# The once-only part of a graph network kernel, cut into 86 pieces that run between the steps of the first graphs

## The reference

```python
# layer 0: pair scores over all nodes, normalised over the whole matrix, leaky relu, softmax over axis 1
e = (x @ a_i)[:, :, None] + (x @ a_j)[:, None, :]
e = leaky((e - mean) * rsqrt(var + eps) * adj + adj);  h = sigmoid(softmax(e, axis=1) @ x)
# layer 1: graph attention, then a GIN step
h = x @ Wp + bp;  s = leaky(h @ a_src [:, None] + h @ a_dst [None, :]);  s = where(adj <= 0, -max, s)
h_gat = relu(layernorm((softmax(s) * adj) @ h));  h_gin = (1 + eps) * h_gat + adj @ h_gat
z = relu(layernorm(h_gin @ W1 + b1));  out = relu(z @ W2 + b2 + h_gat)
# layer 2: weights of the edges from a table e[256], by each edge's number in adj
A = softmax(where(adj > 0, e[number of the edge], NEG), axis=1)
out = (A * eye) @ (x @ W[0]) + (A * (1 - eye)) @ (x @ W[1]) + bias
# layer 3: graph attention with self-loops added to adj
out = elu(softmax(where(adj + eye == 0, -1e9, leaky(e_src + e_dst))) @ (x @ W))
```

## Time and profile before

| | us |
|---|---|
| median of 3 runs | 1245.51 (1245.16 to 1245.55) |
| the profiled execution | 1249.84 |
| its span, first to last instruction | 1248.1 |
| PE busy | 1111.1 (89%) |
| DVE busy | 1096.2 (88%) |
| ACT busy | 1020.0 (82%) |
| POOL busy | 449.1 (36%) |

### The profile page before, as it was taken

One profiled execution on the slowest core, in us unless ns is written; L12 is line 12 of the kernel. 1 busy time (PEld: TensorE's weight loads), 2 busy tenths in 40 slices (PEclk: granted clock), 3 DMA queues, 4 the chain that ended last, 5 costly groups with the idle time before them and its releaser, 6 DMA issues.

```text
span 1248.1 us, 29006 instructions
## 1 busy us (share of the span) xinstructions
PE 1111.1 (89%) x7632; PEld 903.1 (72%) x7632; DVE 1096.2 (88%) x4212; ACT 1020.0 (82%) x2582; POOL 449.1 (36%) x832
## 2 busy tenths in 40 slices
PE   6447889999999999999999999999999999999863
PEld 3235677888777777778877777777888777778753
DVE  5656789999999999999999999999999999998743
ACT  2244679999999888998999988889999999889764
POOL 4002324343334343444333334434443334443320
PEclk9667999999999999999999999999999999999986
DMA  3000001101100111111011011111101100110000
GB/s 64 17 26 9 27 26 35 35 26 34 34 22 20 34 34 34 34 34 34 25 34 33 10 32 34 34 34 34 34 25 34 34 21 21 34 35 26 18 9 17
DMA packets 59460, 35.94 MB, mean 29 GB/s; under 512 B 3873, under 2 KB 54817, under 8 KB 59425
## 3 DMA queue, kind: packets, MB, share of 16 engines
q1 hardware_dynamic: 59424, 35.54, 9.4%
HBM read 18.75 MB, written 8.39 MB: 22 GB/s over the span
## 4 chain that ended last, share of the span: by engine, by line
DVE 37%; PE 21%; issue 20%; POOL 9%; ACT 5%; DVEq 2%; DMA 1%; POOLq 0%; ACTq 0%; SPq 0%
PE ps L792 5%; DVE pTB L954 4%; DVE wE L928 3%; PE ps L761 3%; PE ps L777 3%; DVE vA L1027 3%; PE ps L667 3%; DVE wE L941 2%; DVE vA L1046 2%; POOL lnr_E L593 2%; POOL lnr_B L593 2%; DVE wB L928 2%; PE ps L660 2%; ACT xout L1213 2%; DVE wB L941 2%
## 5 line engine op out<-in xcount | busy, mean ns | idle before, releaser
L777 PE MATMUL ps<-hE,pTE 128*128 128x128 f32 x1024 | 136.4, 277 | 0.0
L708 PE MATMUL ps<-xsA,pA 128*128 128x128 f32 x1024 | 124.0, 280 | 7.4 <-ACT xsA L1268 7.4
L777 PE MATMUL ps<-hB,pTB 128*128 128x128 f32 x1024 | 126.3, 277 | 0.0
L777 PEld LDWEIGHTS ps<-hE,pTE 128*128 128x128 f32 x1024 | 125.0, 193 | 0.6 <-issue 0.4
L708 PEld LDWEIGHTS ps<-xsA,pA 128*128 128x128 f32 x1024 | 118.5, 194 | 9.2 <-ACT xsA L1268 8.3
L792 PE MATMUL ps<-gin_j,hgat 128*128 128x512 f32 x256 | 123.7, 607 | 0.0
L826 PE MATMUL ps<-att_j,xD 128*128 128x512 f32 x256 | 122.8, 603 | 0.0
L777 PEld LDWEIGHTS ps<-hB,pTB 128*128 128x128 f32 x1024 | 120.9, 194 | 0.1
L1258 ACT ACTIVATE pA<-vA,nmA,rirA 128x512 f32<-128x512 f32 x128 | 103.6, 816 | 16.7 <-issue 15.6
L928 DVE SCALAR_TENSOR_TENSOR wE<-ps,hE,y2E 128x512 f32<-128x512 f32 x128 | 94.7, 745 | 25.2 <-ACT y2E L1290 23.7
L1027 DVE CUSTOM_DVE_ANT_0 vA<-ps,adj_j 128x512 f32<-128x512 f32 x128 | 84.8, 682 | 17.7 <-PE ps L695 13.6
(11 more groups left out here) (237 smaller groups left out, 3115.2 us busy)
## 6 DMA issues: line engine op xcount, KB each, us to landing
xA<-in_x_dram SPq DMA_DIRECT2D x32, 256.0 KB, 2.8
xrA<-in_x_dram SPq DMA_DIRECT2D x32, 256.0 KB, 2.6
xrB<-xB SPq DMA_DIRECT2D x32, 256.0 KB, 2.3
out_dram<-xout SPq DMA_DIRECT2D x32, 256.0 KB, 2.2
adj_i<-in_adj_dram SPq DMA_DIRECT2D x1, 1024.0 KB, 5.3
a<-in_L_gnn_a_dram SPq DMA_DIRECT2D x2, 64.0 KB, 4.7
w_sb<-in_L_gnn_W_dram SPq DMA_DIRECT2D x2, 64.0 KB, 3.9
l2w<-in_L_gnn_W_dram SPq DMA_DIRECT2D x2, 64.0 KB, 3.4
```

What stands on the lines that cost most here:

```text
L708: last = mm(at("aggA")[:, i * P:(i + 1) * P], pA[:, j, i * P:(i + 1) * P], xsA[:, j], start=(j == 0), stop=(j == NT - 1))
L777: last = mm(at("agg" + n)[:, i * P:(i + 1) * P], att[n]["pT"][:, i, j], att[n]["h"][:, j, 0:P], start=(j == 0), stop=(j == NT - 1))
```

## The change

The first block, the clearing of semaphores and the barrier are gone. Every part of the once-only work is now a named piece in the lists of the second block: `t.once(piece, it)` runs it in turn `it` alone. 86 pieces stand among the steps of turns 0 to 4.

```diff
+    def once(self, part, it):
+        if isinstance(self.it, int) and self.it == it:
+            part(Once(self))
...
-        with ExitStack() as setup_ctx:
-            s = Signals()
-            block = setup_ctx.enter_context(nc.Block())
...
-        nc.clear_and_free_semaphores(list(s.values()))
-        nc.all_engine_barrier()
```

The pieces of one engine count on one semaphore. `SETUP` lists their signals in the engine's order, `after(name, n)` gives the value to wait for. Only steps of the first graph (`g.first`) wait for pieces, each for those that it reads:

```diff
+        def after(name, n):
+            eng = SETUP_ON[name]
+            return s["setup_" + eng], [k + 1 for k, x in enumerate(SETUP[eng]) if x == name][n - 1]
...
             def dots_A(c):
                 def step(g):
+                    if g.first:
+                        dve.wait_ge(s["a_in"], 32)
...
                 def h_tiles(name, which):
                     def step(g):
+                        if g.first:
+                            pe.wait_ge(*after("wx_ready", 4))
+                            pe.wait_ge(*after("brows_ready", 3))
...
             def v_A(j):
                 def step(g):
+                    if g.first:
+                        dve.wait_ge(*after("adjT_copied", NT))
...
             def ax_D(half):
                 def step(g):
+                    if g.first:
+                        pe.wait_ge(*after("att2T_copied", NT))
```

Two pieces as examples, and the pieces and moved steps of DVE's list as far as the prediction names them:

```diff
+            def transpose_w(once):
+                pe.wait_ge(s["weights_in"], 16 * N_LOADS)
+                bank_free(once, "wT")
+                nc.tensor.transpose(at("wT", P), wx1[:, 0:P], ident[:])
+                nc.tensor.transpose(at("wT")[:, P:2 * P], wx3[:, 0:P], ident[:]).then_inc(*signal("wT_in_psum"))
+            def totals(once):
+                dve.wait_ge(*after("counts_in_psum", NT))
+                for i in range(NT):
+                    v.tensor_copy(tot[:, i:i + 1], at(f"count{i}")[:, N - 1:N]).then_inc(*signal("tot_ready"))
...
+                t.once(edge_ranks, 1)
...
+                t.once(no_edge_B, 0)
                 t.run(join_A, 1)
...
                 t.run(shift_A, 0)
+                t.once(split_rest0, 1)
+                t.once(normal_rows0, 2)
...
+                t.once(match_edges1, 1)
+                t.once(normal_rows1, 2)
                 t.run(L_E1, 4)
+                t.once(bias_row1, 1)
                 t.run(M_E0, 4)
+                t.once(normal_rows2, 2)
                 t.run(M_E1, 4)
+                t.once(split_low, 1)
+                t.once(past_table1, 1)
                 t.run(L_E2, 4)
+                t.once(mask_adj, 0)
+                t.run(L_E3, 4)
+                t.once(row_minimum3, 2)
+                t.run(M_E2, 4)
                 t.run(v_A0, 0)
-                t.run(M_E2, 4)
+                t.once(bias_row2, 1)
                 t.run(v_A1, 0)
...
                 t.run(lrelu_A2, 0)
+                t.once(totals, 0)
                 t.run(lrelu_A3, 0)
+                t.once(normal_rows3, 2)
...
                 t.run(M_B0, 1)
-                t.run(M_B1, 1)
-                t.run(recip_E, 4)
+                t.once(copy_w, 0)
                 t.run(y_D, 3)
```

More of the change, by code:

```diff
@@ L290, in _ @@
                     sp.dma_start(dst, src).then_inc(s["weights_in"], 16)
[L292 to L331, removed]
@@ new lines, in _, with offsets @@
+            count0, count1, count2, count3 = (count(i) for i in range(NT))
+            def offsets(once):
+                pe.wait_ge(*after("tot_ready", NT))
+                pe.wait_ge(*after("above_set", 1))
+                bank_free(once, "offsets")
+                mm(at("offsets", NT), above[:], tot[:], start=True, stop=False, skip_group_check=True)
+                for t in range(NT - 1):
+                    last = mm(at("offsets")[:, t + 1:NT], ones[:], tot[:, t:t + 1].to_broadcast([P, NT - 1 - t]), start=False,
+                              stop=(t == NT - 2), skip_group_check=True)
+                last.then_inc(*signal("off_in_psum"))
@@ new lines, in fetch_counts, with part @@
+            def fetch_counts(c):
+                def part(once):
+                    pe.wait_ge(*after("sel_ready", 1))
+                    pe.wait_ge(*after("cnt_ready", NT))
+                    bank_free(once, f"edge{c}")
+                    for i in range(NT):
+                        last = mm(at(f"edge{c}"), sel_i[:, i, c * P:(c + 1) * P], cnt[i], start=(i == 0), stop=(i == NT - 1))
+                    last.then_inc(*signal("edges_in_psum"))
+                return part
+            fetch_counts0, fetch_counts1 = (fetch_counts(c) for c in range(EC))
@@ new lines, in match_edges, with part @@
+            def match_edges(c):
+                def part(once):
+                    dve.wait_ge(*after("edges_in_psum", c + 1))
+                    dve.wait_ge(*after("kin_ready", 1))
+                    dve.wait_ge(*after("neg_ready", 2))
+                    v.tensor_scalar(q_k[:, c], at(f"edge{c}"), kin[:, c:c + 1], ecol[:, c:c + 1], ALU.is_equal,
+                                    ALU.mult).then_inc(*signal("q_ready"))
+                return part
+            match_edges0, match_edges1 = (match_edges(c) for c in range(EC))
@@ L893, in stats_of @@
+            normal_rows0, normal_rows1, normal_rows2, normal_rows3 = (normal_rows(i) for i in range(NT))
             def stats_of(k, src=None):
```

744 lines of the change are left out of this document (491 added, 253 removed), and 11 rows, old and new, of the table IN_BANK.

## The result

The changed kernel takes 1239.93 us (median of 9 runs, 1239.05 to 1245.84) against 1247.37 for the kernel before (9 runs, 1245.16 to 1252.96). The ratio is 0.9939, 95% interval 0.9918 to 0.9960: 0.6% faster. The forecast was 1207.0 with a range of 1191 to 1226. Direction right, size wrong, by 33 us.

The account below looks back on a forecast made before the run. VectorE and TensorE were taken as both nearly full in the loop, with once-only work and pipeline fill before it. -39.9 + 5.0 + 3.5 + 1.0 - 8.1 = -38.5 from 1245.51 gave 1207.0 us, range 1191 to 1226.

Parts of the forecast that it names:

- Turn 0: Start to y_A of graph 0: prA starts at 5.0 us, y_A comes at 35.0, 39.9 earlier than 74.86.
- the weights' wait: Turn 0, TensorE: weight transposes wait for all loads until 18.5 us; counts queued behind end at 23.3, over 1 us later.
- Turns 1 to 3: Turns after graph 0's y_A: once-only work partly covered, costing +5.0, +3.5 and +1.0 us.
- The loop: 27 loop turns: new order wins 0.3 us a turn, -8.1 in all; bounds -21 and +9.
- diag_D moves too: Loop, POOL: M_E2 loses its 0.35 us, offset_B pays the same; counted as nothing, bounds -0.35 and +0.35 a turn.
- the -8.1: Loop: 27 turns at 0.3 us won each, from the waits for y2E and before vA.
- The signs named in advance: Wrong if y_A of graph 0 after 40, turn 1 over 40, or loop turn over 34.6 (look for who waits for rowsA).
- The -0.3 for y2E and v_A: Loop, VectorE: waits of 0.28 for y2E and 0.14 before vA go; 0.3 of 0.42 us a turn taken as won.
- Slower: Loop, ScalarE: relu_B and norm_E in front of copy_rowsA cost from 1.13 us a turn; 1256 at 1.5; chance 0.03.
- It doesn't do what it says: Front: a piece heading TensorE's queue holds the first graph; only the seam's idle 4.95 us is won, 1240.5; chance 0.03.
- a rival's value: Nothing is covered: once-only pieces in turns 1 and 2 cost in full, loop gains 0; -19, 1226 us; chance 0.09.

Follow-up runs that it names:

- e8: Changed kernel with diag_D waiting for M_E2 (beside v_A), triangles early in turn 0, and load_a in front of load_xA: 1214.95 us, 0.9733 of the kernel before.
- e5: Changed kernel with diag_D behind rstd_A and waiting for M_E2, so xTdD runs beside v_A: 1219.03 us, 0.9757 of the kernel before.
- e10: Kernel before the change with only M_E2 and v_A1 exchanged on VectorE: 1240.51 us, 0.9914 of the kernel before.
- e12: Changed kernel with xTdD in two halves, the first behind power_A, the second late beside v_A: 1223.78 us, 0.9779 of the kernel before.
- e9: The kernel of e8 with diag_D's wait for M_E2 left out from turn 32 on: 1214.08 us, 0.9692 of the kernel before.
- e6: Changed kernel with POOL's triangles moved in turn 0 from behind power_A to behind the iotas: 1240.90 us, 0.9940 of the kernel before.

## Why the prediction was wrong

- **Turn 0: right within 4 us, in part by luck.** 38.8 for 35.0. The a loads landed at 7.9, not 5.0 (+2.9). cenA and r1A lost 1.7 each to POOL's triangles, which the step did not have. On the other side, no_edge_B took 1.2 instead of the 2.8 of the earlier trace rows. VectorE waited for the counts in front of tot as forecast, but only 0.8, and not because of the weights: their transposes started at 22.84, when the pair matmuls let them. With the weights' wait the step had the right mechanism too early: it shows in e8, where the chain is shorter.
- **Turns 1 to 3: right in sum.** +6.6 for +9.5; somewhat more was covered than I had let. No run took the cover of a single piece apart.
- **The loop: wrong, in the paragraph "diag_D moves too".** The step priced the new place of xTdD by the row of M_E2: it "reads two SBUF tensors as M_E2 does, so I let it pay the same and count nothing", with offset_B as the victim and +0.35 as the upper bound. The timeline of the kernel before held the right reading; behind xTdD, 663.27 to 664.54, it has

```profile
664.06 1.03 DVE L941 CUSTOM_DVE_ANT_0 wE<-wE,no_i 128x512 f32<-128x512 f32 x1
```

  When M_E2 started, 0.48 us of xTdD were left, and M_E2 lost 0.35. The 0.35 was the rest of a POOL instruction, not a price of M_E2. At the new place the victim starts 0.06 us behind xTdD, so 1.20 of 1.26 is left, and it lost 1.00. The first instruction behind power_A is shift_A and not offset_B, and the two POOL and VectorE instructions are started by the same event, so they meet in every turn. The term should have been 27 x (1.0 - 0.35) = +17.6 instead of nothing. With the -8.1 that did not come either (next point) that is 26 of the 33 us missed. Another 5 come from the step from the profile to the median: I took 4.3 off, and the changed kernel's profiled execution lay 0.9 under its median. The last 2 are spread over the front, the drain and the first turns of the loop. The signs named in advance caught it only in part: the turn was over 34.6, but the place to look was said to be rowsA, and t2B, which should have gone to 1.03, stayed at 0.69.
- **The -0.3 for y2E and v_A: wrong as well.** The wait for y2E went as forecast, but e5, without it and with no VectorE instruction held up by xTdD, takes 34.17, and e10, with most of it, 34.10: its removal was worth nothing. A wait for euE of the same size (0.28 a turn) stands in its place.
- **The rivals.** None had POOL and VectorE in it. "Slower" put the loss into ScalarE's list, in front of copy_rowsA; nothing on VectorE waited for rowsA. "It doesn't do what it says" gives 1240.5, and 1239.93 was measured; that is luck, since its mechanism would have lost the front, and the front was won. The range ended at 1226, a rival's value; in the bounds this term had 0.35 a turn. With 1.26 a turn, the duration of xTdD itself, as its upper bound, the forecast and this term alone (1207 + 34) would have reached 1241.
- **The rule cited beside it.** It named the partners (two SBUF inputs, or a 2-port mode), and the runs agree: cenA, r1A, spA, t2B and M_E2 wait, v_A and L_E, which read PSUM and only one tensor in SBUF, do not. The step took the rule for a price that goes with the VectorE instruction, when it only says who can meet. The Trainium skill says more than I drew on (SBUF — State Buffer, Who interferes with whom): the pair of ports is an exclusive lock, whoever issues first holds it for the whole instruction and the other blocks fully. The trace agrees, for xTdD: shift_A ends 0.03 us behind it, and takes 0.68 beside a POOL instruction of 0.72 (e12). For POOL's narrow instructions it does not (last section), and there the measurement decides.

## What to carry to other kernels

When a POOL instruction on whole tiles is moved, list the VectorE instructions that will start while it runs. If POOL's instruction reads SBUF, charge the first of them that has two inputs in SBUF, or is a tensor_scalar or a cast within SBUF, with what is left of POOL's instruction (here less 0.13 to 0.21 us), however small its own work is. If it only writes, as a memset, a tensor_scalar and a cast waited here, and prA with two inputs did not. Other kinds of VectorE instructions were not put beside xTdD. Worst is a POOL instruction directly behind one that VectorE waits for, because the same event starts both. Best is to put it beside VectorE instructions that read PSUM, with a wait if the order does not do it; and such a wait belongs only where its cover exists (the drain took 116.3 us with it in e5, 110.8 without it in e9).

A short instruction that "takes" 1.2 us is a wait that no view of waits shows: compare each tile's median with that of the kernel before.

## What was not expected of the hardware

POOL can be the one that waits, too. rstd_Z's first instruction on POOL, four numbers a partition, took 0.56 us before and 1.29 in the changed kernel, where it starts 0.05 us behind the first of two lrelu_A of VectorE (together 1.28). POOL's instructions of tile lnve_Z, before and then after:

```profile
L587 POOL TENSOR_TENSOR lnve_Z<-lnmv_Z,consts x10: 553/556/557, 532.8 to 843.2; 128x4 f32<-128x4 f32 x10
```

```profile
L437 POOL TENSOR_TENSOR lnve_Z<-lnmv_Z,consts x10: 1288/1288/1289, 510.6 to 827.1; 128x4 f32<-128x4 f32 x10
```

The same form takes 0.20 on tile lnve_D. So it was held up before as well, there until 0.06 us behind the end of the first of two lrelu_A, though the second had begun; in the changed kernel both had to end. Why it got in between them in one and not in the other is open.

The time of a POOL instruction does not say how long it holds VectorE up. lnr_B on POOL takes 1.05 us for four numbers a partition, and prA on VectorE, with two inputs in SBUF, runs beside it at its usual 0.28 (tile prA, ten turns: 279/284/306):

```profile
527.90 1.05 POOL L443 TENSOR_TENSOR lnr_B<-lnve_B,consts 128x4 f32<-128x4 f32 x1
...
528.23 0.28 DVE L1180 SCALAR_TENSOR_TENSOR prA<-xA,a 128x128 f32<-128x128 f32 x1
```

Those that held VectorE up for all that was left of them were wide: 128x2048 and 128x512, 128x256 in e12, and the 128x128 of tile xE that gives cenA its 0.42 in e6. And a memset of 128x2048, which reads nothing, held up the tensor_scalar shift_A in turn 0 for its whole 1.81 us.
